# Short products of constants on TensorE around the router logits of three expert stages, and ahead of one stage's blocks

## What is computed

```python
# layer 0: 8 experts, the best 2 of a token, at most int(1.2 * T / 8) tokens for an expert
probs = jax.nn.softmax(xf @ gate_w.T + gate_b, axis=-1)
...
# layer 1: 8 experts, the best one of a token
router_logits = xf @ Wr + br
...
# layer 3: 32 experts, each takes its best k = 39 tokens
h = xf @ W_router + b_router
Sm = jax.nn.softmax(h, axis=-1)
G_ek, idx_ek = jax.lax.top_k(Sm.T, k)
```

## Time and profile before

| | us |
|---|---|
| median of 3 runs | 3022.14 (3017.99 to 3024.03) |
| the profiled execution, as timed | 3048.43 |
| its span | 3046.7 |
| PE busy | 2483.3 |
| DVE busy | 1641.0 |
| ACT busy | 861.9 |
| POOL busy | 590.4 |

### The profile page before, as it was taken

How to read it: one execution, slowest core, us unless ns; L and a number is a source line. 1 busy time by engine, 2 the same in 40 slices (tenths; PEclk the granted TensorE clock), 3 DMA queues, 4 the chain that set the end, 5 groups by cost and what they waited for, 6 DMA issues and landing times. The chain is left out here.

```text
span 3046.7 us, 30957 instructions
## 1 busy us (share of the span) xinstructions
PE 2483.3 (82%) x10585; PEld 1585.0 (52%) x10585; DVE 1641.0 (54%) x3721; ACT 861.9 (28%) x1943; POOL 590.4 (19%) x566
## 2 busy tenths in 40 slices
PE   4877965999956888785577999999999879768896
PEld 1344444999943667673453455344554334544442
DVE  9999344222334888886235898618962532531000
ACT  2165110111111666663111465105631100110110
POOL 0000046354403444430110000000001001022211
PEclk9999976999977888887598999999999989779998
DMA  4000445767824554550534453214534121569996
GB/s 129 0 1 1 141 103 159 236 200 236 269 69 119 147 141 132 147 122 22 188 118 151 182 188 116 85 60 159 172 109 136 39 95 47 187 216 352 343 340 192
DMA packets 198728, 445.53 MB, mean 146 GB/s; under 512 B 26570, under 2 KB 48058, under 8 KB 198094
## 3 DMA queue, kind: packets, MB, share of 16 engines
q1 hardware_dynamic: 156942, 344.67, 33.8%
q0 software_dynamic: 41632, 98.89, 12.5%
HBM read 396.77 MB, written 49.05 MB: 146 GB/s over the span
## 5 line engine op out<-in xcount | busy, mean ns | idle before, releaser
L2169 PE MATMUL psum<-x_res,HH 125*128 125x512 f32 (+1 forms) x960 | 351.5, 525 | 19.7 <-DVE x_res L2359 19.7
L2169 PEld LDWEIGHTS psum<-x_res,HH 125*128 125x128 f32 x960 | 181.3, 193 | 179.1 <-issue 156.6
L1147 POOL DMA_INDIRECT recd<-edge_records,edge_slots x160 | 193.7, 1211 | 328.0 <-issue 321.7
L1514 POOL DMA_INDIRECT hg<-HT,srcidx x196 | 191.0, 974 | 299.7 <-PE psum L1634 163.4
L1634 PE MATMUL psum<-hg,Dh 128*125 128x258 f32 x784 | 232.9, 462 | 4.6 <-DVE ACC L1577 1.8
L1675 ACT ACTIVATE hg<-hg,ex 128x129 f32<-128x129 f32 x784 | 235.1, 388 | 1.6
L2159 PE MATMUL psum<-W,XO 128*125 128x512 f32 x480 | 209.0, 596 | 0.0
L1634 PEld LDWEIGHTS psum<-hg,Dh 128*125 128x125 f32 x784 | 177.8, 233 | 45.9 <-issue 3.7
L2938 PE MATMUL psum<-wd,XN 128*40 128x512 f32 (+1 forms) x704 | 166.9, 632 | 42.3 <-DMA wd<-in_L_ffn_W_down 42.3
L1181 PE MATMUL psum<-xgT,w 128*128 128x192 f32 x1024 | 174.1, 329 | 2.5 <-DMA w<-in_L_ffn_w 2.5
L1181 PEld LDWEIGHTS psum<-xgT,w 128*128 128x128 f32 x1024 | 167.5, 191 | 6.7 <-DMA w<-in_L_ffn_w 3.7
(11 more groups left out here) (509 smaller groups left out, 3974.6 us busy)
## 6 DMA issues: line engine op xcount, KB each, us to landing
wd<-in_L_ffn_W_down SPq DMA_DIRECT2D x30, 2560.0 KB
w<-in_L_ffn_w SPq DMA_DIRECT2D x64, 1024.0 KB, 12.3
MK<-CT SPq DMA_DIRECT2D x80, 625.0 KB
wu<-in_L_ffn_W_up SPq DMA_DIRECT2D x8, 2730.0 KB, 20.3
rows<-ROWS POOLq DMA_DIRECT2D x24, 625.0 KB, 7.4
w<-in_L_ffn_W SPq DMA_DIRECT2D x18, 512.0 KB
t<-in_L_ffn_tv_W SPq DMA_DIRECT2D x16, 512.0 KB
targets<-DROW SPq DMA_DIRECT2D x49, 128.0 KB
```

Of the source, the lines that this page charges most:

```text
L1147: pool.indirect_dma_start(out=g.recd, out_offset=bass.IndirectOffsetOnAxis(ap=g.posi[:, c:c + 1], axis=0), in_=g.E8[:, c, :], in_offset=No ...
L1514: pool.indirect_dma_start(out=hg[j % RING][:, c, :], out_offset=None, in_=g.HT, in_offset=bass.IndirectOffsetOnAxis(ap=g.srcidx[:, j * CH ...
L2169: return pe.matmul(flat[:, at:at + x1 - x0], HH[:, k, h * DH + c * 128:h * DH + c * 128 + 128], z[n % 4][:, x0:x1], start=(k == 0 and i < ...
```

## The change

A helper issues products of the bf16 identity with itself, repeated to 512 columns, into bank 7. Nobody reads the result. Six of them stand ahead of the first tile of each front, two behind each tile's logits, and eight ahead of the blocks of R1, behind a new wait of PE for the ten scatters.

```diff
+def keep_clock(g, out, times):
+
+    for _ in range(times):
+        g.nc.tensor.matmul(out, g.identb[:], g.identb[:, None, :].to_broadcast([128, out.shape[1] // 128, 128]),
+                           start=True, stop=True)
...
@@ Router.pe_products
         ins.then_inc(*self.norm.used.up())
+        keep_clock(g, g.PS[:, 7, :], 2)
 
     def pe_logits(self):
+        keep_clock(self.g, self.g.PS[:, 7, :], 6)
         self.norm.pe_program(self.pe_products)
...
@@ ffn1, pe_program
             pe.wait_ge(*weights.at(32 * NE))
             pe.wait_ge(*experts.at(1))
+            pe.wait_ge(*scattered.at(16 * NT))
+            keep_clock(g, g.PS[:, 7, :], 8)
             for j in range(SB + 2):
```

## The result

The changed kernel takes 3026.23 us (median of 10 runs, 3024.10 to 3030.03). The kernel before, in 10 runs on the same chip, takes 3019.55 us (3015.76 to 3024.03). The ratio is 1.0024, with a 95% interval of 1.0016 to 1.0032: 7.3 us slower, between 4.8 and 9.7. I had forecast 10.2 us.

What follows compares the result with a forecast made beforehand. TensorE at half clock was taken to bound the three fronts, on one barrier-closed chain of stages; 8.1 + 8.1 - 1 - 5 = +10.2 us, carried over to the runs' median of 3022.14, gave 3032 us, range 3021 to 3049.

Steps and rivals of the forecast that it cites:

- The likeliest case: Fronts of R0 and R1 at half clock, R3 at full: 7 to 16 us longer, 3029 to 3039; chance 0.60.
- R0, +8.1: Front with two experts per token: six products hide, pairs behind tiles 1 to 9 cost 0.9 us each, +8.1 us.
- R1's front, +8.1: Front with one expert per token: six products hide, pairs behind tiles 0 to 8 cost 0.9 each, +8.1 us.
- My nearest row: Price of a pair at half clock: clearing products before R0's first expert, 0.96 us a pair; 0.9 taken.
- R1's blocks, -1: Eight products delay the first transposes 0.8 to 1.2 us but raise the clock sooner: net -1 us (-2 to +1.2).
- R3, -5: Front with 32 experts: clock rises, tile 1.71 us against 2.41, logits 6 us sooner; net -5 us (-6.5 to -2).
- I take 1: R3's token gather, issued sooner, meets the weights' loads filling the DMA engines: 1 us of the gain lost.
- the other bound that I had named: R3's gather loses all of the 4 us or so by which it comes too early.
- The rise in R3: Six products running into eight transposes, some 4.3 us without a gap, raise the clock to full; about 3 in 4.
- a rival with 0.22: Half clock everywhere, all three fronts: R3 costs +9.5, in all +24.7 us, 3047; chance 0.22.
- Rival 3: Pairs lift and hold the clock in fronts of R0, R1 and R3: -18 us, 3004; chance 0.10, with partial cases.

Runs made afterwards that it cites:

- The held loads: Kernel before plus R3's products, SP holding the first group's second pair of down weights until its gathers land: 0.9962; same hold without any products: 1.0002.
- the two filled kernels: Changed kernel with 24 products ahead of R1's first tile, 30 behind R0's tile 0; elsewhere pairs (1.0013 to before) or one per tile (0.9980).

## Why the prediction was right

The likeliest case happened: half clock in R0 and R1, full in R3, slower by more than 0.2%. The rise of 7.3 us is at the low end of this case's 7 to 16, and the median of 3026.23 lies below its own 3029 to 3039, and only inside the wide range of 3021 to 3049. It is 5.8 us below the forecast of 3032. The base accounts for 2.6 of it (before's median over 10 runs is 3019.55, over the first three 3022.14), the sum for the rest. That the sum came so near is in part luck: the pairs were put 2.7 us too dear and the loss at the gather 2.6 us too cheap, which cancel. Term by term:

- **R0, +8.1: measured +6.6**, and **R1's front, +8.1: measured +6.9.** The mechanism was right: the pairs behind nine tiles on a full PE, at 0.50, the six hidden. The size was off: a pair costs 0.77 us of period, not 0.9 (3.18 against 2.41), and 9 x 0.77 = 6.9. My nearest row, the clearing products at 0.96, overstated it, and so did twice the full-clock price.
- **R1's blocks, -1: measured -2.2 from the one trace to the other, -1 over the means of the table, -1.5 (-4.6 to +1.5) by itself.** The first transposes were not late by 0.8 to 1.2 us but by less than 0.1, since the eight started half a microsecond sooner than I had put them and took 3.2 us, and the clock was up as they began.
- **R3, -5: measured -3.0.** The front gave what I had worked out: the gather is issued 6.6 us sooner, against 6, a period of 1.66 against 1.71. The step that failed is "I take 1" for what is lost at the gather. It was 3.6, near the other bound that I had named. The held loads show it by intervention: with them the wait is 7.23 again, and without a raised front they give nothing. The selection that I put at 20 us is 30 (from the front's end at 2656.2 to 2686.76); the sum did not use it.
- **The rise in R3.** I had argued from 4.3 us of six products and eight transposes together. The rise did come (4.5 us behind the six's start), and the pairs without the six never brought it. But the windows of R1 show that six products alone raise the clock, so the part of the transposes in it is not shown by R3. By the Trainium skill ("TensorE: Matmul & The Clock Gate", Part 4: PE-mode transpose) transposes do not count as busy in the same way, and I had let that rule stand for a rival with 0.22 and half clock everywhere (+24.7). The rival did not come. My step from the rule to half clock was wrong in any case: that the six would stand alone does not keep the clock down, as R1's six show (1.00 from 1448.20). Whether the rule is wrong is left to the rows at 896.03 and 900.20, which speak against it; the rise behind six products agrees with either.
- **Rival 3, the pairs lift the clock in all fronts.** It needed tiles with a pair, begun at half clock, to rise. They did not in any of three fronts, 27 to 32 us long (R0 and R1 of the changed kernel, R3 without the six). Even with the clock up for most of the front, R0 gave 0.8 to 1.7 us and not 5 (the two filled kernels at 95.1 and 94.1): I had left out that its stores would hold DVE back at the faster pace, though I had named the store that DVE waits for.

## What to carry to other kernels

Filler work on an engine whose clock follows its activity pays only where it leads into the real work without a gap; in the changed kernel, six products ended a front 6.4 us sooner that followed at once, pairs included, and gave nothing where 5 to 7 us of idleness came between. Filler inside a stretch in which the engine is already full cost its whole length at the low clock, and in R3 it was not needed at the high one. Filling the idle gap itself raised the clock in some executions and not in others. And an edit that brings a small gather forward has to be read together with the bulk loads that it now meets: holding back two experts' weights kept the gain.

## What the runs showed of the hardware

- R3's tiles, busy without a gap and mostly with loads for narrow fp32 products, kept the clock at which they began: 32.00 of 32.00 us at 0.50 with pairs (without the six), 12.00 of 12.00 us at 1.00 without them (with the six). The same tiles take 2.41 us each in before and 1.26 with the six ahead. This is not so of all busy work: transposes at 896.03 began at 0.50 and rose.
- Six bf16 products of 128 x 512, 2.72 us behind a long idle stretch, were followed by 1.00 while PE did nothing (1448.20 to 1451.20), and by 0.50 again before the next work at 1453.13.
- Two bf16 products of 128 x 512 cost 0.77 to 0.81 us at half clock and 0.40 to 0.43 at full, by periods.
- Four gathers of 40 rows, issued by the same code, kept PE waiting for 7.2 to 7.3 us in every kernel where they were late or the loads were held (DMA share 0.18), and 10.3 to 11.5 us where they were issued 7 to 11 us sooner among the weight loads (share 1.04 in the changed kernel).
